# Convolution weights mixed from pairs of shifts on 128 partitions

## What is computed

```
a = softmax(alphas)
w_total = a[0] * weight
for idx, bs in enumerate([2, 4, 8, 16]):
    tmp = weight in blocks of bs x bs
    compress = mean over r of tmp[:, :, r, (r + c) % bs]
    w_total = w_total + a[idx + 1] * (compress laid out as a circulant of bs x bs)
x = x + conv3x3(groupnorm(x), w_total)
```

## Time and profile before

| what | value |
|---|---|
| median of 3 runs | 2620.75 us (2616.24 to 2620.89) |
| the profiled execution, its own time | 2618.04 us |
| its span, first to last instruction | 2616.2 us |
| busy share of the span: PE, DVE, ACT, POOL | 46%, 72%, 26%, 66% |
| chain that ended last, by engine | POOL 39%, DVE 23%, PE 19%, issue 15% |

### The profile page before, as it was taken

One profiled execution on the slowest core, in us unless ns is written; L12 is line 12 of the kernel. 1 busy time (PEld: TensorE's weight loads), 2 busy tenths in 40 slices (PEclk: granted clock), 3 DMA queues, 4 the chain that ended last, 5 costly groups with the idle time before them and its releaser, 6 DMA issues.

```text
span 2616.2 us, 34056 instructions
## 1 busy us (share of the span) xinstructions
PE 1201.4 (46%) x12499; PEld 1006.1 (38%) x12499; DVE 1874.7 (72%) x3127; ACT 682.7 (26%) x696; POOL 1719.7 (66%) x1690
## 2 busy tenths in 40 slices
PE   4874000001110101000003499689889899898486
PEld 2532000001000000000002355379889889898366
DVE  7588596999779998887207600168888888888556
ACT  1010002434353534343300111222222222222221
POOL 0001877777777777777777577777777777777370
PEclk9977555555555555555555555579989999899658
DMA  9500213333232332333321606121221222211101
GB/s 300 201 1 23 72 38 101 110 100 97 83 111 87 102 104 94 100 100 131 108 48 33 94 7 189 24 25 26 26 41 26 25 41 26 40 26 26 29 9 34
DMA packets 145714, 186.75 MB, mean 71 GB/s; under 512 B 84844, under 2 KB 103982, under 8 KB 139166
## 3 DMA queue, kind: packets, MB, share of 16 engines
q1 hardware_dynamic: 91494, 121.12, 14.6%
q0 software_dynamic: 54080, 63.61, 12.9%
HBM read 97.32 MB, written 87.32 MB: 71 GB/s over the span
## 4 chain that ended last, share of the span: by engine, by line
POOL 39%; DVE 23%; PE 19%; issue 15%; ACT 1%; SPq 1%; DMA 1%; DVEq 1%; POOLq 0%; ACTq 0%
POOL arena L728 35%; DVE arena L1367 10%; PE psum L1053 9%; DVE arena L1370 7%; PE psum L935 2%; POOL d_adseed L818 2%; DVE arena L1977 2%; DVE arena L1928 2%; PE psum L1014 2%; PE psum L1026 2%; PE psum L904 2%; POOL d_qseed L752 2%; PE psum L1098 1%; SPq L569 1%; PE psum L1129 1%
## 5 line engine op out<-in xcount | busy, mean ns | idle before, releaser
L1367 DVE TENSOR_TENSOR arena<-arena 128x512 f32<-128x512 f32 (+17 forms) x1331 | 766.2, 615 | 210.3 <-DMA arena<-d_ac,arena 65.7
L728 POOL DMA_INDIRECT arena<-d_h,arena x668 | 643.6, 963 | 226.7 <-issue 199.6
L728 POOL DMA_INDIRECT arena<-in_kv,arena x640 | 662.8, 1036 | 195.0 <-issue 195.0
L1053 PE MATMUL psum<-arena 128*128 128x128 bf16 x10080 | 615.7, 225 | 90.2 <-DVEq L1975 88.1
L1053 PEld LDWEIGHTS psum<-arena 128*128 128x128 bf16 x10080 | 602.2, 101 | 95.1 <-DVE arena L1370 91.9
L851 PE MATMUL psum<-arena 128*128 128x128 f32 (+3 forms) x402 | 91.1, 395 | 1021.3 <-DVEq L1443 791.1
L851 PEld LDWEIGHTS psum<-arena 128*128 128x128 f32 (+3 forms) x402 | 69.8, 205 | 1043.8 <-DVEq L1443 806.5
L1370 DVE TENSOR_SCALAR arena<-arena 128x512 bf16<-128x512 f16 (+8 forms) x1067 | 334.1, 371 | 72.6 <-ACT arena L1273 28.8
L1367 DVE TENSOR_TENSOR arena<-psum,arena 128x512 f32<-128x512 f32 (+2 forms) x179 | 141.2, 796 | 210.2 <-PE psum L1014 202.6
L728 POOL DMA_INDIRECT arena<-d_adst,arena x40 | 54.3, 1357 | 257.6 <-DVEq L1614 245.7
L1014 PEld LDWEIGHTS psum<-arena 128*128 128x128 f32 x512 | 113.7, 328 | 146.9 <-issue 110.5
(11 more groups left out here) (190 smaller groups left out, 1518.8 us busy)
## 6 DMA issues: line engine op xcount, KB each, us to landing
d_gs<-arena SPq DMA_DIRECT2D x32, 768.0 KB, 4.5
d_as<-arena SPq DMA_DIRECT2D x20, 1152.0 KB, 4.4
d_qseed<-arena SPq DMA_DIRECT2D x5, 4096.0 KB, 29.6
arena<-d_qseed SPq DMA_DIRECT2D x20, 1024.0 KB, 5.1
arena<-d_h,arena POOLq DMA_INDIRECT x668
arena<-in_kv,arena POOLq DMA_INDIRECT x640, 2.5
d_adseed<-arena SPq DMA_DIRECT2D x1, 4096.0 KB, 29.7
arena<-d_adseed SPq DMA_DIRECT2D x17, 128.0 KB
```

The source lines that it names most:

```text
L728: return pool.indirect_dma_start(out, None, table, bass.IndirectOffsetOnAxis(index[:, t:t + 1], 0))
L1053: last = nc.tensor.matmul(ps[2 + turn_of(b, m)][:, k * PICK_W:(k + 1) * PICK_W], pick_hot[turn_of(b, m)][:, t, k * P:(k + 1) * P], h_split ...
L1367: return V.tensor_tensor(o, a_, b_, op)
```

## The change

The 30 shifts are taken two at a time. `w_dup` now fills 128 partitions: the upper 64 hold the same blocks as the lower 64, turned by one more position, and `perm` holds on the upper 64 the permutation of the odd shift. One product then contracts over 128 partitions and adds two shifts, so that a part has 15 products in place of 30. The host writes the doubled rows, and one transfer of 128 rows of 18,432 bytes stands for the eight. `alphas` goes to all 128 partitions and its arrival is counted on `const_in`; the mixing now waits for `w_in` itself. In `between`, `mix_maximum` moves from behind merge 3 to behind merge 2, and `mix_permutations` from behind merge 4 to behind merge 3.

```diff
-N_SHIFT = sum(BLOCKS)
+N_PAIR = sum(BLOCKS) // 2
...
-            perm[m // bs * bs + (m % bs - k) % bs, n, :, m] = 1.0
-            n += 1
-    return c, perm.reshape(CH, (1 + N_SHIFT) * P)
+            perm[k % 2, m // bs * bs + (m % bs - k) % bs, n + k // 2, :, m] = 1.0
+        n += bs // 2
+    return c, perm.reshape(P, (1 + N_PAIR) * P)
+
+def doubled_blocks(w):
+    halves = []
+    for by in range(2):
+        parts = []
+        for bs in BLOCKS:
+            b = w.reshape(CH // bs, bs, CH // bs, bs, TAPS).transpose(2, 1, 0, 3, 4)
+            if by:
+                b = np.concatenate([b[:, :, :, -1:], b[:, :, :, :-1]], axis=3)
+            b = np.ascontiguousarray(b).reshape(CH, CH // bs, 1, bs * TAPS)
+            parts.append(np.concatenate([b, b], axis=2).reshape(CH, 2 * CH * TAPS))
+        halves.append(np.stack(parts, axis=1))
+    return np.ascontiguousarray(np.concatenate(halves, axis=0)).reshape(P, len(BLOCKS) * 2 * CH * TAPS)
...
-            sp.dma_start(alph[0:CH, 0:5], io["alphas"].partition_broadcast(CH)).then_inc(w_in, 16)
+            sp.dma_start(alph[:, 0:5], io["alphas"].partition_broadcast(P)).then_inc(const_in, 16)
...
-            sp.dma_start(perm[0:CH, :, :].rearrange("p n m -> p (n m)"), io["perm"]).then_inc(perm_in, 16)
+            sp.dma_start(perm.rearrange("p n m -> p (n m)"), io["perm"]).then_inc(perm_in, 16)
...
-            for n, bs in enumerate(BLOCKS):
-                view = w_dup[0:CH, n, :].rearrange("p (q s b) -> p q s b", s=2, b=bs * TAPS)
-                for copy in range(2):
-                    sp.dma_start(view[:, :, copy, :],
-                                 io["w_blocks"][n].rearrange("p (q b) -> p q b", b=bs * TAPS)).then_inc(w_in, 16)
+            sp.dma_start(w_dup.rearrange("p b n -> p (b n)"), io["w_blocks"]).then_inc(w_in, 16)
...
             pe.wait_ge(perm_scaled, 1)
+            pe.wait_ge(w_in, 32)
...
-                    for k in range(bs):
+                    for k in range(0, bs, 2):
                         lo = (bs - k) % bs * TAPS
-                        last = nc.tensor.matmul(acc, perm[0:CH, n, :], view[:, part * q:(part + 1) * q, lo:lo + bs * TAPS],
-                                                start=False, stop=n == N_SHIFT)
+                        last = nc.tensor.matmul(acc, perm[:, n, :], view[:, part * q:(part + 1) * q, lo:lo + bs * TAPS],
+                                                start=False, stop=n == N_PAIR)
...
-                dve.wait_ge(w_in, 16 * 10)
-                al = alph[0:CH]
+                dve.wait_ge(const_in, 32)
+                al = alph
...
-                    ins = ts(perm[0:CH, n:n + bs, :], perm[0:CH, n:n + bs, :], al[:, m + 1:m + 2], ALU.mult, 1.0 / bs, ALU.mult)
-                    n += bs
+                    ins = ts(perm[:, n:n + bs // 2, :], perm[:, n:n + bs // 2, :], al[:, m + 1:m + 2], ALU.mult, 1.0 / bs, ALU.mult)
+                    n += bs // 2
...
-            between = {3: (norm_means, mix_maximum), 4: (norm_spread, mix_permutations), 5: (norm_variance,), 6: (norm_scale,)}
+            between = {2: (mix_maximum,), 3: (norm_means, mix_permutations), 4: (norm_spread,), 5: (norm_variance,), 6: (norm_scale,)}
```

More of the change, by code:

```diff
@@ L97, in shape_constants @@
         c[:, C_TOGGLE + m] = (sign[m] if m < 7 else 1.0) * (sign[m - 1] if m else 1.0)
-    perm = np.zeros((CH, 1 + N_SHIFT, 2, CH), np.float32)
+    perm = np.zeros((2, CH, 1 + N_PAIR, 2, CH), np.float32)
     m = np.arange(CH)
-    perm[m, 0, :, m] = 1.0
+    perm[0, m, 0, :, m] = 1.0
     n = 1
@@ L373, in build @@
         square_a = y_pad.rearrange("p j y x -> p (j y x)")[:, 0:NT * CH // 2].rearrange("p (i c) -> p i c", c=CH)
-        perm = c.take((1 + N_SHIFT) * P).rearrange("p (n m) -> p n m", m=P)
+        perm = c.take((1 + N_PAIR) * P).rearrange("p (n m) -> p n m", m=P)
         a = Region(mid)
@@ L915, in tokens @@
                 last.then_inc(t_turned, 1)
-            pe.wait_ge(const_in, 16)
+            pe.wait_ge(const_in, 32)
             pe.wait_ge(gn_pair_in, 1)
@@ L1136, in _ @@
             act.wait_ge(alpha_exp_in, 1)
-            nc.scalar.activation(alph[0:CH, 8:13], alph[0:CH, 0:5], ACT.Exp).then_inc(alpha_exp, 1)
+            nc.scalar.activation(alph[:, 8:13], alph[:, 0:5], ACT.Exp).then_inc(alpha_exp, 1)
             act.wait_ge(gn_ready, 1)
@@ L1416, in mix_permutations @@
                 step(ts(al[:, 0:5], al[:, 8:13], al[:, 15:16], ALU.mult))
-                ts(perm[0:CH, 0, :], perm[0:CH, 0, :], al[:, 0:1], ALU.mult)
+                ts(perm[0:CH, 0, :], perm[0:CH, 0, :], al[0:CH, 0:1], ALU.mult)
                 n = 1
                 for m, bs in enumerate(BLOCKS):
-                    ins = ts(perm[0:CH, n:n + bs, :], perm[0:CH, n:n + bs, :], al[:, m + 1:m + 2], ALU.mult, 1.0 / bs, ALU.mult)
-                    n += bs
+                    ins = ts(perm[:, n:n + bs // 2, :], perm[:, n:n + bs // 2, :], al[:, m + 1:m + 2], ALU.mult, 1.0 / bs, ALU.mult)
+                    n += bs // 2
                 step(ins)
@@ L1735, in _ @@
             step(ins)
-            dve.wait_ge(const_in, 16)
-            between = {3: (norm_means, mix_maximum), 4: (norm_spread, mix_permutations), 5: (norm_variance,), 6: (norm_scale,)}
+            dve.wait_ge(const_in, 32)
+            between = {2: (mix_maximum,), 3: (norm_means, mix_permutations), 4: (norm_spread,), 5: (norm_variance,), 6: (norm_scale,)}
             for k, merge in enumerate(A_MERGES, 1):
@@ L2187 @@
         "w_own": np.ascontiguousarray(w.transpose(1, 0, 2)).reshape(CH, CH * TAPS),
-        "w_blocks": np.stack([np.ascontiguousarray(
-            w.reshape(CH // bs, bs, CH // bs, bs, TAPS).transpose(2, 1, 0, 3, 4)).reshape(CH, CH * TAPS) for bs in BLOCKS]),
+        "w_blocks": doubled_blocks(w),
         "kv": np.concatenate([given("L1_attn_k", (A_NODES, CH)), given("L1_attn_v", (A_NODES, CH))], axis=1),
```

2 lines of the change are left out of this document (1 added, 1 removed).

## The result

| what | before | after |
|---|---|---|
| median of 4 runs | 2620.07 us (2616.24 to 2620.89) | 2585.62 us (2581.71 to 2588.86) |
| ratio of the times, 95% interval | | 0.987 [0.9858, 0.9882] |
| the profiled execution, its own time | 2618.04 us | 2584.71 us |
| its span | 2616.2 us | 2582.9 us |

A forecast was written before the change was run, and what follows sets the result against it. The end hung on the early chain to the first `conv_add`, with DVE stalls of 8.0 and 28.3 us; gains of 37.4 (slow mixing) and 36.9 us (fast) gave 37 off 2618.04, 2581.0, stated as 2582 for scatter; range 2575 to 2590.

The forecast's parts named there:

- The stalls: DVE's waits before `mix_maximum` (8.0 us) and the first `conv_add` (28.3 us) go; DVE reaches `conv_add` at 75.1, not 84.38.
- The landing of `x`: Start of DVE's work: `x` stays at 17.04, and `mix_maximum` fills 0.33 us of the 0.59 us wait for it.
- PE's start and the weights: Mixing starts at 31.8 instead of 40.4, after the small product; weights land at 28.4, leaving 3.4 us of cover.
- The rival at 127 GB/s: Weights' transfer lands late, PE starts at 41.1; with slow mixing the gain is 28.1 us, time 2590; chance 9%.
- The mixing: PE's 64 remaining instructions take 31.1 us at 0.48 us each, or 15.4 us at 0.24, against 59.9 before.
- The slower second convolution: After PE idles 11 us, `conv(1)` takes 10.64 us instead of 7.90; 2.5 of 2.7 us covered, 0.7 estimated lost.
- Moves the rest of the span as a whole.: Everything behind the first `conv_add` at 112.70 shifts with it; `conv_add` to POOL's start stays 139.7 us.
- the fast case: Mixing at 0.24 us per instruction, DVE arriving last at 75.1: gain 37.6 us, 36.9 net; chance 45%.
- The hidden gain: Rival: POOL or the queue sets the gathers' start, so time stays 2618 and 37 us become a new wait; 3%.
- The zeros: Rival: zeros share the transfer engines, weights land at 90, `conv_add` comes at 133.5, time 2639; chance 3%.
- point of decision, 69.2: Zeros rival: weights' landing from which the change loses, 112.7 less 43.5 us from landing to first `conv_add`; earlier still gains.

The follow-up runs named there:

- the run with the weights at 43.8: Changed kernel with the weights' one transfer queued behind the second graph's edges and one write of zeros: 2586.57 us, one execution.
- the products on 64 partitions: Changed kernel with its 15 shifted products of a part over the lower 64 partitions alone, odd shifts left out: 2590.78 us, ratio 0.9895.
- the weights behind five writes: Changed kernel with the weights' one transfer queued behind the second graph's edges and five of six writes of zeros: 2626.27 us, ratio 1.0026.
- the order alone: Kernel before with only the moved pieces in `between`, `alphas` counted on `const_in` and PE waiting for the weights itself: 2610.59 us, ratio 0.997.
- each pair twice: Changed kernel with every shifted product over 128 partitions issued twice, so each shift is added twice: 2576.56 us, one execution.

## Why the prediction was right

The forecast was 2582 us, 37 us gained; measured were 2585.62 and 34.5. By its steps:

- **The stalls.** Right: both are gone, and DVE arrives by its own work. The prediction had `conv_add` at 75.1; it came at 76.18. From the statistics to merge 4 DVE took 27.36 - 18.12 = 9.24 us, forecast 26.3 - 17.04 = 9.3.
- **The landing of `x`.** This term was mis-sized. The prediction kept `x` at 17.04 and let `mix_maximum` fill part of the 0.59 us of waiting; `x` came at 18.12 and DVE waited 1.34 us. That is the 1.1 us by which `conv_add` is late. It is not shown to be scatter alone: one program varied by 1.9 us, but every profile with pairs where DVE waited for `x` had it later than both profiles without, and the wider load of `alphas` ahead of it, which the prediction passed over, is not tested. The prediction also called `perm` no larger than it was; it is 1,024 KB and was 992, without effect, since it landed at 21.3.
- **PE's start and the weights.** Right: the small product releases the mixing, at 32.80 (forecast 31.8; the later `x` accounts for the difference). The weights landed at 28.2; the prediction took 28.4, by 398 GB/s. The rival at 127 GB/s, 41.1, did not come, and at the pace found even that would have been free, as the run with the weights at 43.8 shows.
- **The mixing.** The two bounds were 15.4 and 31.1 us; it took 19.7, near the fast end, since its first part began at the lower level. The Trainium skill, "TensorE: Matmul & The Clock Gate", Part 1, says that sustained matmul activity releases the low clock. The products on 128 partitions agree with this, at 0.25 us in the second part; the unbroken products on 64 partitions, at 0.48 us over two blocks of 29 us, still do not.
- **The slower second convolution.** The size was right at the second `conv_add`, the cause only in part. After 15.13 us without work PE ran the transposes at 77.31 and 79.50 in 1.33 us each, and `conv(1)` in 9.53 us instead of 7.90. The two `conv_add` lie 91.10 - 76.18 = 14.92 us apart, before 127.00 - 112.70 = 14.30: 0.62 us lost, estimated were 0.7. With the products on 64 partitions, where PE idled 1.24 us ahead of the transposes, the distance was 91.22 - 76.92 = 14.30 again. But a long gap is not needed for a slow `conv(1)`: with the weights behind five writes PE had also idled only 1.24 us, and `conv(1)` took 9.32 us, the distance being 132.10 - 117.54 = 14.56; with the order alone it took 9.54 us, at 14.41. By POOL's start no loss is to be seen: from `conv_add` to there were 139.4 us, 138.9 to 139.9 in all other profiles, where 139.7 were asked for.
- **"Moves the rest of the span as a whole."** This held up to POOL's start and is not shown beyond it. At POOL's start 36.8 us were won; at the end of the profiled span 33.3, and 34.5 of the medians. That 36.8 meets the 36.9 of the fast case is in part luck: `conv_add` came 36.5 us sooner and not 37.6, because of `x`, and the 0.7 us put down for the second convolution did not turn up at POOL. The 3.5 us between POOL and the end are within the 13 us by which the way from the first gather to the end differs among the runs, but this width hangs on a single kernel, each pair twice; the other profiles with pairs all lose there. The prediction named such a rearrangement and put it into the range, 2575 to 2590, but not into the point.
- **The rivals.** The hidden gain did not come, POOL's wait shrank with DVE's work. The zeros did not overtake: the weights landed at 28.2. A landing that late does cost, as forced above: weights that land at 89 make the kernel slower than before. This rival's point of decision, 69.2, was worked out with the slow mixing; with 28.5 us from landing to `conv_add` it is 112.70 - 28.5 = 84.2.

## What to carry to other kernels

A chain of products that contract over 64 partitions can be folded into half as many on 128 when the operands come from the host; ask then which engine is late next, since here 14 of the microseconds saved only became slack of PE. Once the stall was gone, what only gave PE more slack (order, earlier transfer, faster pace) was worth less than 1 us at the instruction that had waited, and it is cheaper to see that in the idle time ahead of the waiting instruction than in the total. A gain at the start of a kernel need not arrive whole at its end: here 36.8 us at POOL's first gather were 33.3 at the end, and the runs do not tell whether scatter or the change took the rest.

## What the hardware showed unexpectedly

**The width of the products went with the clock.** The profile prints the granted clock as 1.00 for all of the mixing, slow or fast, so the pace of the rows has to tell it. In the mixing's second part 30 instructions (15 products) of 288 columns took 14.60 us on 64 partitions and 7.56 us on 128, in otherwise equal programs; 0.49 and 0.25 us per instruction are the paces of 1.2 and 2.4 GHz, as `conv(0)` of before showed them one after the other. In the change PE went up within the first part, after it had begun with products of 128 partitions. The stretches of PE's line L947 in the kernel after (busy us, instructions, granted clock, DMA share, GB/s):

```profile
34.00:36.00 2.00, 1.95 (x4) 1.00 1.05 410
...
40.00:42.00 2.00, 2.00 (x10) 1.00 1.05 408
```

Four in 2 us, and then ten. At its start an instruction over 128 partitions thus cost what one over 64 did, 0.49 us. The Trainium skill, "TensorE: Matmul & The Clock Gate", "Why this matters for your kernels", says of narrow products that one over 32 partitions takes the time of one over 128. At one clock these rows agree for 64. Over the whole mixing they do not, since on 64 partitions the pace stayed at 0.49 us.

It fell again when PE had little to do. All engines in two later stretches (busy us and instructions of PE, its weight loads, DVE, ACT and POOL, then granted clock, DMA share, GB/s):

```profile
60.00:70.00 10.00, 2.18 (x6) 0.62 (x4) 9.58 (x27) 0.00 (x0) 0.00 (x0) 0.84 1.04 398
70.00:80.00 10.00, 1.83 (x8) 1.43 (x8) 8.40 (x21) 0.80 (x2) 0.00 (x0) 0.50 1.03 383
```

PE's last product of the first convolution had ended at 62.2. With the weights behind five writes the clock fell without such a gap, behind the transposes that follow the first `conv_add`; a stretch of that kernel, in the same columns:

```profile
122.00:125.00 3.00, 3.00 (x5) 1.20 (x4) 2.62 (x9) 0.24 (x1) 0.00 (x0) 0.59 0.00 0
```

**The landing of `x` is not repeatable.** The same two transfers came at 17.04 and 17.67 in the two kernels without pairs, and between 18.05 and 20.01 in the eight others whose DVE waited for them, with and without other transfers queued behind; two profiles of one program had 18.12 and 19.99. They came late where `alphas` ahead of them took longer. What sets it was not found.
